# An adaLN block with linear attention and a mixture of experts: the opening reordered, and the output product in plain f32

## The reference

```
mod = silu(c) @ wmod                         # c: [4, 256], wmod: [256, 6*256]
sa, ca, ga, sb, cb, gb = six slices of mod   # one row of 256 per batch entry
ga, gb = sign * max(|.|, 0.25)
h = layernorm(x) * (1 + ca) + sa             # x: [4, 2048, 256]
q, k, v = h @ w_qkv.T, in 16 heads of 16;  q, k = elu(q)+1, elu(k)+1
S_t = S_{t-1} + k_t v_t^T;  z_t = z_{t-1} + k_t          # causal linear attention
o_t = (S_t q_t) / max(z_t q_t, 1e-6);  x = x + ga * (o @ w_out.T)
h = layernorm(x) * (1 + cb) + sb
top-2 of 8 experts (w_router), capacity 1280 rows each, gates renormalised
x = x + gb * sum_e combine_e * (silu(h @ w_gate.T) @ w_down[e].T)
```

## Time and profile before

| | |
|---|---|
| median of 3 runs | 967.09 us (965.5 to 968.11) |
| profiled execution | 968.82 us, span 967.1 us |
| mean granted TensorE clock | 0.962 of 2.4 GHz |
| PE, PEld busy | 880.2 us, 738.5 us |
| DVE, ACT, POOL busy | 644.7, 496.4, 515.3 us |

### The profile page before, as it was taken

The page is one execution under the profiler, slowest core; times in us unless marked ns, Lnnn a source line. Parts: engine busy times, 40 slices in busy tenths (PEclk is TensorE's granted clock), DMA queues, the critical chain, the costliest instruction groups (busy, mean ns, idle before and its releaser), DMA issues.

```text
span 967.1 us, 23422 instructions
## 1 busy us (share of the span) xinstructions
PE 880.2 (91%) x8232; PEld 738.5 (76%) x8232; DVE 644.7 (67%) x1869; ACT 496.4 (51%) x1002; POOL 515.3 (53%) x641
## 2 busy tenths in 40 slices
PE   4899999999999999999999999981099999999994
PEld 2677877777777777777787777751099999999994
DVE  4466587777867867778768677765056755677752
ACT  3645656655556555555565565332065555455541
POOL 3212435656556656565556564545535765566564
PEclk9899999999999999999999999995599999999998
DMA  9984012223222322222123211212156766676663
GB/s 320 338 268 106 2 45 89 67 90 95 59 87 65 103 93 65 87 75 58 64 50 76 56 36 44 52 29 72 53 144 148 153 128 138 142 140 142 135 110 43
DMA packets 70981, 98.36 MB, mean 102 GB/s; under 512 B 7794, under 2 KB 52850, under 8 KB 70792
## 3 DMA queue, kind: packets, MB, share of 16 engines
q1 hardware_dynamic: 37912, 52.09, 19.5%
q0 software_dynamic: 21760, 31.66, 14.9%
q10 hardware_dynamic: 11248, 13.81, 4.4%
HBM read 46.84 MB, written 63.36 MB: 114 GB/s over the span
## 4 chain that ended last, share of the span: by engine, by line
PE 80%; issue 5%; DVE 5%; POOL 4%; DMA 4%; ACT 1%; DVEq 0%; POOLq 0%; ACTq 0%; SPq 0%
PE SCW L1163 13%; PE SCW L1394 9%; PE PJ L1255 9%; PE OB L1196 7%; PE MD L1229 5%; PE OB L1187 5%; PE MA L1409 5%; PE MD L1409 4%; PE PJ L1265 4%; PE SB L1209 4%; PE MD L1173 3%; PE MA L1222 2%; DMA out<-EX,desti 2%; PE PJ L1280 2%; POOL slot_rows L480 2%
## 5 line engine op out<-in xcount | busy, mean ns | idle before, releaser
L825 DVE TENSOR_TENSOR Sm<-SCW,tri 128x1024 f32<-128x1024 f32 x128 | 156.1, 1220 | 75.5 <-PE SCW L1163 75.5
L480 POOL DMA_INDIRECT slot_rows<-Hrow,sloti x128 | 126.8, 991 | 43.2 <-issue 43.1
L1163 PE MATMUL SCW<-QM,KT 32*128 32x256 f32 x1024 | 144.9, 400 | 0.8 <-DVE Sm L825 0.3
L538 POOL DMA_INDIRECT out<-EX,desti x80 | 127.2, 1590 | 32.6 <-issue 32.2
L496 POOL TENSOR_TENSOR X<-X,og 128x256 f32 (+1 forms) x64 | 46.8, 731 | 174.8 <-DVE og L1024 174.2
L1163 PEld LDWEIGHTS SCW<-QM,KT 32*128 32x128 f32 x1024 | 87.7, 184 | 35.6 <-issue 19.6
L1255 PE MATMUL PJ<-hT,w_qkv 128*128 128x512 f32 x384 | 107.2, 417 | 6.1 <-POOL hT L490 6.1
L608 ACT ACTIVATE EX<-PJ 128x512 f32<-128x512 f32 x64 | 38.2, 597 | 103.3 <-PE PJ L1255 103.3
L1255 PEld LDWEIGHTS PJ<-hT,w_qkv 128*128 128x128 f32 x384 | 70.0, 195 | 18.4 <-issue 6.3
L490 POOL TENSOR_TENSOR hT<-N,hT 128x512 fp32r<-128x512 f32 x32 | 41.6, 1321 | 75.1 <-ACT hT L595 75.1
L1196 PE MATMUL OB<-Sm,VA 128*17 128x128 f32 x2048 | 81.1, 276 | 0.0
(11 more groups left out here) (191 smaller groups left out, 1986.7 us busy)
## 6 DMA issues: line engine op xcount, KB each, us to landing
Hrow<-slot_rows SPq DMA_DIRECT2D x32, 516.0 KB, 4.1
slot_rows<-erow ACTq DMA_DIRECT2D x1, 10400.0 KB, 52.4
X<-x SPq DMA_DIRECT2D x16, 512.0 KB, 4.9
out<-X SPq DMA_DIRECT2D x16, 512.0 KB
Hrow<-mod_rows SPq DMA_DIRECT2D x16, 512.0 KB, 8.0
QT<-slot_rows SPq DMA_DIRECT2D x8, 516.0 KB, 3.7
slot_rows<-Hrow,sloti POOLq DMA_INDIRECT x128, 2.8
N<-wd SPq DMA_DIRECT2D x4, 512.0 KB, 5.5
```

What stands on the lines that cost most here:

```text
L480: pool.indirect_dma_start(xe, bass.IndirectOffsetOnAxis(sloti[:, k, t:t + 1], 0), Hrow[:, 1 - gp, t, :], None, bounds_check=SLOTS - 1, oob ...
L538: pool.indirect_dma_start(out, bass.IndirectOffsetOnAxis(desti[s % 2][:, a:a + 1], 0), Ys[s % 2][:, a, :], None, bounds_check=TOK - 1, oob ...
L825: dve.tensor_tensor(o.rearrange("p c (k w) -> p c k w", k=2), SCW[:].rearrange("p k (c w) -> p c k w", c=DC), tri[:].rearrange("p k i -> p ...
L1163: last[k] = mm(SC[k][:, cc * 2 * P:(cc + 1) * 2 * P], KT[rows, gp, cc, q * P:(q + 1) * P], QM[rows, tp, :, cc, :], start=True, stop=True)
```

## The change

Seven things change.

1. Loads. `wmod` is loaded in two pieces: the columns of sa and ca on ScalarE's queue, the other two thirds on SP's queue between the two `X` loads. `wqkv` has a semaphore of its own, and is no longer behind the wait for `w_r`'s zeroing.
2. The slot fill is issued by ScalarE in its slot j = 4 instead of before Silu. Silu waits for `c` alone.
3. TensorE enters the slots after the columns of sa and ca; the modulation's four rows are made after the first group's transposes (j = 4), into PSUM banks `OB` and `SB` instead of the score banks, and VectorE copies them out after the low parts of `hT`.
4. The first group's low parts (`hT[:, 1]`) are made by VectorE instead of GpSimd.
5. ScalarE copies `saca` out after the first four norms (j = 3) instead of before `w_qkv`'s high part.
6. The output product uses plain f32: `ATs` and `w_o` have one part each, two matmuls instead of six; `attention_lo` is gone, as are `w_o`'s high and low part in the opening.
7. `mod12`, `tmp`, `sgn` and the experts' second block buffer lie elsewhere (`VS` is new); two waits for them fall away.

```diff
@@ buffers
-        ATs = sb("ATs", [P, 2, DC, P], F32R)
+        ATs = sb("ATs", [P, DC, P])
-        w_o = sb("w_o", [P, 2, DC, D], F32R)
+        w_o = sb("w_o", [P, DC, D])
+        VS = sb("VS", [P, 2, DC, BW], F32R)
-        mod12 = Smf[0:BATCH, DC * 6 * D:(DC * 6 + 4) * D].rearrange("p (k d) -> p k d", k=4)
-        tmp, sgn = (EX[0:BATCH, i, :].rearrange("p (k d) -> p k d", k=2) for i in range(2))
+        tmp, sgn = (KT[0:BATCH, 1, i, :].rearrange("p (k d) -> p k d", k=2) for i in range(2))
+        mod12 = Hf[0:BATCH, 2048:2048 + 4 * D].rearrange("p (k d) -> p k d", k=4)
@@ run_slots
-                    if early and it == -1 and j == early_at:
-                        early()
+                    if early and it == -1:
+                        early(j)
@@ SP
             sp.dma_start(X[:, 0:GT, :], xg[0]).then_inc(x_in[0], 16)
+            sp.dma_start(wmod_sb[:, :, 2 * D:6 * D], wmod[:, :, 2 * D:6 * D]).then_inc(wm_in[1], 16)
             sp.dma_start(X[:, GT:2 * GT, :], xg[1]).then_inc(x_in[1], 16)
...
-            sp.wait_ge(w_lo, 2)
+            sp.wait_ge(w_lo, 1)
@@ GpSimd
-                if q == 0 and group_ok(gn + 1):
+                if q == 0 and group_ok(gn + 1) and gn >= 0:
@@ ScalarE
             act.dma_start(cT[:], c).then_inc(c_in, 16)
-            act.dma_start(wmod_sb, wmod).then_inc(c_in, 16)
+            act.dma_start(wmod_sb[:, :, 0:2 * D], wmod[:, :, 0:2 * D]).then_inc(wm_in[0], 16)
+            act.dma_start(w_qkv_raw, wqkv).then_inc(wq_in, 16)
             act.wait_ge(wr_zero, 1)
-            for dst, src in ((w_qkv_raw, wqkv), (w_o_raw, wo), (w_r[:, :, 0:E], wr), (w_g_raw, wg)):
+            for dst, src in ((w_o[:], wo), (w_r[:, :, 0:E], wr), (w_g_raw, wg)):
                 act.dma_start(dst, src).then_inc(w_in, 16)
-            act.wait_ge(consts, N_CONST)
-            act.dma_start(xe[:, 0:D + 4]..., erow[:].to_broadcast(...)).then_inc(init_out, 16)
-            act.wait_ge(c_in, 32)
+            act.wait_ge(c_in, 16)
             act.activation(cS[:], cT[:], ACT.Silu).then_inc(c_silu, 1)
...
+            act.wait_ge(wq_in, 16)
+            act.activation(w_qkv[:, 0], w_qkv_raw, ACT.Copy).then_inc(w_hi, 1)
+            def early(j):
+                if j == 3:
+                    act.wait_ge(mod_mm, 1)
+                    (the two saca copies)
+                    act.wait_ge(mod_ev, 2)
+                if j == 4:
+                    act.wait_ge(w_in, 48)
+                    act.activation(w_g[:, 0], w_g_raw, ACT.Copy).then_inc(w_hi, 1)
+                    act.wait_ge(consts, N_CONST)
+                    act.dma_start(xe[:, 0:D + 4]..., erow[:].to_broadcast(...)).then_inc(init_out, 16)
...
-                if n_next == 0 and m == 0:
-                    act.wait_ge(gate_fix, 5)
@@ VectorE
+            def early(j):
+                if j == 0:
+                    (the parity column)
+                if j == 1:
+                    dve.wait_ge(w_hi, 1)
+                    (the low part of w_qkv)
+                if j == 4:
+                    for cidx in range(DC):
+                        dve.wait_ge(h_hi, cidx + 1)
+                        dve.tensor_tensor(hT[:, 1, cidx, :], hT_raw[:, cidx, :], hT[:, 0, cidx, :].bitcast(F32),
+                                          ALU.subtract).then_inc(h_lo, 1)
+                    dve.wait_ge(mod_mm, 3)
+                    (mod12 from OB and SB, then the clamping of the gates, as before)
+                if j == 7:
+                    dve.wait_ge(gate_fix, 5)
+                    dve.wait_ge(w_hi, 2)
+                    (the low part of w_g)
-                if tile_ok(n - 1):
-                    attention_lo(T)
@@ TensorE
             pe.wait_ge(c_silu, 1)
+            pe.wait_ge(wm_in[0], 16)
...
+            def early(j):
+                if j == 4:
+                    modulation(0)
+                    modulation(1)
+                if j == 7:
+                    pe.wait_ge(w_in, 48)
...
             def out_product(T):
-                pe.wait_ge(at_lo, T)
+                pe.wait_ge(at_done, T)
                 for cc in range(DC):
-                    for i, (ap, wp) in enumerate(SPLIT):
-                        last = mm(MD[:, 0:D], ATs[:, ap, cc, :], w_o[:, wp, cc, :], start=(cc + i == 0),
-                                  stop=(cc == DC - 1 and i == len(SPLIT) - 1))
+                    last = mm(MD[:, 0:D], ATs[:, cc, :], w_o[:, cc, :], start=(cc == 0), stop=(cc == DC - 1))
                 last.then_inc(op_full, 1)
```

More of the change, by code:

```diff
@@ L174, in adaln_block @@
         XT = [a.rearrange("p (k c n) -> p k c n", k=2, c=DC)
-              for a in (KS[:].rearrange("p k c n -> p (k c n)"), w_o[:].rearrange("p k c n -> p (k c n)"))]
+              for a in (KS[:].rearrange("p k c n -> p (k c n)"), VS[:].rearrange("p k c n -> p (k c n)"))]
         Ys = [EXf[:, i * 512:(i + 1) * 512].rearrange("p (a n) -> p a n", a=2) for i in range(2)]
@@ L790, in _ @@
             dve.memset(VA[:], 1.0).then_inc(dve_setup, 1)
[L791 to L816, removed]
@@ L818, in _ @@
-            SC0m, SC1m = (SC[k][0:BATCH, :].rearrange("p (k d) -> p k d", k=2) for k in range(2))
+            def early(j):
+                if j == 0:
+                    dve.wait_ge(consts, N_CONST)
+                    dve.tensor_reduce(parity[:, 0:1], pairmask[:], AX_X, ALU.add).then_inc(gate_fix, 1)
+                    dve.wait_ge(gate_fix, 1)
+                    dve.tensor_scalar(parity[:, 1:2], parity[:, 0:1], -1.0, 1.0, ALU.mult, ALU.add).then_inc(dve_setup, 1)
+                if j == 1:
+                    dve.wait_ge(w_hi, 1)
+                    dve.tensor_tensor(w_qkv[:, 1], w_qkv_raw, w_qkv[:, 0].bitcast(F32), ALU.subtract).then_inc(w_lo, 1)
+                if j == 4:
[4 more added lines that the diff above has]
+                    dve.wait_ge(mod_mm, 3)
+                    dve.tensor_copy(mod12[:, 0:2, :], OBm).then_inc(gate_fix, 1)
+                    dve.tensor_scalar(mod12[:, 2, :], SBm[:, 0, :], 1.0, None, ALU.add)
+                    dve.tensor_copy(mod12[:, 3, :], SBm[:, 1, :]).then_inc(gate_fix, 1)
+                    dve.wait_ge(gate_fix, 3)
+                    gate = mod12[:, 0:4:3, :]
+                    dve.scalar_tensor_tensor(tmp, gate, -1.0, gate, ALU.mult, ALU.max)
+                    dve.tensor_scalar(sgn, gate, 0.0, 2.0, ALU.is_ge, ALU.mult).then_inc(gate_fix, 1)
+                    dve.wait_ge(gate_fix, 4)
+                    dve.tensor_scalar(tmp, tmp, 0.25, None, ALU.max).then_inc(mb_ev, 1)
+                    dve.wait_ge(mb_ev, 1)
+                    dve.scalar_tensor_tensor(gate, sgn, -1.0, tmp, ALU.add, ALU.mult).then_inc(gate_fix, 1)
+                if j == 7:
+                    dve.wait_ge(gate_fix, 5)
+                    dve.wait_ge(w_hi, 2)
+                    dve.tensor_tensor(w_g[:, 1], w_g_raw, w_g[:, 0].bitcast(F32), ALU.subtract).then_inc(w_lo, 1)
@@ L820, in masked_scores @@
+            OBm, SBm = (a[0:BATCH, :].rearrange("p (k d) -> p k d", k=2) for a in (OB, SB))
             def masked_scores(T, pair, tp, n):
@@ L1141, in _, with modulation @@
             last.then_inc(mod_mm, 1)
-            for hh in range(2):
+            pe.wait_ge(dve_setup, 2)
+            pe.wait_ge(consts, N_CONST)
+            def modulation(hh):
+                if hh == 0:
+                    pe.wait_ge(wm_in[1], 16)
                 for k in range(DC):
-                    last = mm(SC[hh][0:BATCH, :], cS[:, k, :], wmod_sb[:, k, (2 + 2 * hh) * D:(4 + 2 * hh) * D],
+                    last = mm((OB, SB)[hh][0:BATCH, :], cS[:, k, :], wmod_sb[:, k, (2 + 2 * hh) * D:(4 + 2 * hh) * D],
                               start=(k == 0), stop=(k == DC - 1))
                 last.then_inc(mod_mm, 1)
-            pe.wait_ge(w_in, 64)
-            pe.wait_ge(dve_setup, 2)
-            pe.wait_ge(consts, N_CONST)
+            def early(j):
[4 more added lines that the diff above has]
+                    pe.wait_ge(w_in, 48)
             def scores(T, q, gp, tp, pair):
-                if isinstance(T, int) and T == 0 and pair == 0:
-                    pe.wait_ge(gate_fix, 3)
                 if pair == 0:
@@ L1246, in stage1_qk @@
                 if isinstance(G, int) and N == 0 and m == 0:
-                    pe.wait_ge(w_lo, 2)
+                    pe.wait_ge(w_lo, 1)
                 if m == 0:
```

38 lines of the change are left out of this document (17 added, 21 removed).

## The result

| | before | after |
|---|---|---|
| median (runs) | 967.66 us (6, 965.5 to 968.87) | 979.13 us (6, 974.78 to 984.58) |
| ratio, 95% interval | | 1.0128 (1.0092 to 1.0164) |
| profiled execution, its span | 968.82, 967.1 us | 983.63, 981.8 us |
| granted clock, mean | 0.962 | 0.958 |
| QK of group 0 starts | 27.02 | 21.03 |

The changed kernel is slower by 12.4 us by the ratio (8.9 to 15.9); the forecast was +9.0. In the two profiled executions the span grew by 14.7 us: 3.1 up to tile 2, 7.8 from tile 2 to tile 63, -0.5 from there to the experts, and 4.2 in the expert stage, which the diff does not touch except for one buffer's place. Without it the stages give 10.4 us, inside the interval of the ratio.

What follows compares the result with a forecast made beforehand. TensorE's instruction stream was taken to bound the attention stage, with waits only at its opening and end. +9.9 (tile loop) - 0.7 (end of attention) - 0.2 (opening) = +9.0 us on 967.09, so 976.1 us; range 968.5 to 982.

Steps and rivals of the forecast that it cites:

- TensorE's stream sets the loop: Attention tile loop: the stage is as long as TensorE's instruction stream, so freeing VectorE there buys nothing.
- The product, +9.9 a kernel: Output product in the tile loop: plain f32 costs +0.155 us in each of 64 tiles, +9.9 us (8.3 to 11.5).
- The -0.7 for the end of attention: End of attention: TensorE's two waits for `ATs` fall away, -0.7 us, bounds 0 and -1.5.
- The estimate after the Trainium skill: Output product: true FP32 as four passes, eight 256-column passes against six, 0.21 us more a tile, 13.6 us in all.
- The opening up to tile 0: Opening: QK starts at 22.1, 4.9 us earlier, and first scores come at 30.8, 7.7 us ahead.
- Rival 3: Opening: first piece of `wmod` lands with the whole, modulation at low clock, full 2.8 us paid; 981.9 us, chance 0.14.
- What is late next: Opening after tile 0: gate rows leave later, group 2 lands at 45.4, VectorE waits; 1.6 of 7.7 us are left.
- I keep 19.8: SP's queue in the opening: group 2 lands 19.8 us after the gate rows' store, as before.
- The clock: Opening, after TensorE's wait from about 42: the low clock costs 1.4 us, half of 2.8.
- The opening as a whole: Whole opening: -1.6 + 1.4 = -0.2 us (from -5 to +3).
- Rival 1: Opening: group 2 lands before 38 us, VectorE never waits, low clock not met again; 967.1 us, chance 0.12.
- Rival 4: Opening: it keeps 4.5 us, with gate rows at 23; 971.8 us, chance 0.20.

Runs made afterwards that it cites:

- pad: The changed kernel with VectorE again making one subtraction of 128x256 per tile, into a buffer nobody reads; 980.33 us, ratio 1.014.
- after_again: The changed kernel unchanged, run again beside other kernels on one chip; 981.24 us, ratio 1.0134.
- late_fill: The changed kernel with the slot fill issued after ScalarE's slot n = 2 instead of in j = 4; 968.63 us, ratio 0.9996.
- keep_busy: The changed kernel with 28 extra fp32r matmuls, result never read, on TensorE right before tile 1's second scores; 978.96 us, ratio 1.0126.

## Why the prediction was right, and which of its terms were off

It said 976.1, range 968.5 to 982, slower with 0.81; 979.13 came, 3.0 us more. The mechanism was the one forecast; two terms were off, in opposite directions.

- **TensorE's stream sets the loop: right.** 58 of 61 slots grew, in every quarter, and pad shows that VectorE's time was worth nothing.
- **The product, +9.9 a kernel: a slot is right, the sum too large.** The plain pass was put at 0.217 us; the successive starts give 0.215, and a slot grows by 0.15, as forecast. The step that was off is "Every one of the 64 tiles pays, as TensorE waits for nothing there". Three slots did not pay: the last two had waited for the low part, and the one from tile 23 to 24 for `An` (0.61 us). Together they give back 1.0 us inside the loop, where they would have paid 0.5. The list of waits behind the earlier trace rows has the wait for `An` (0.6 us, once), in a line that was not used; the second of the last two slots, where the product came 0.26 us late, is not in it at all. The -0.7 for the end of attention came as -0.4. Net the product is 7.7 us by the traces (7.9 in the loop, 0.2 ahead of it, -0.4 behind), against 9.2. The 4.0 us wait for `pos` in the earlier trace rows is the quarter-slot's own and did not change. The estimate after the Trainium skill, "FP8 and Floating Point Precision", TensorE Precision Notes, put the term at 13.6. Its four passes are borne out in their cost (two instructions of 0.215 us for 256 columns); it came out high since it took the fp32r passes at a bare 0.107 us where the rows have 0.118.
- **The opening up to tile 0: right.** QK at 21.03 (22.1), first scores at 29.86 (30.8). `wqkv` had landed at 10.1, 1.4 us sooner than assumed; the modulation's rows took 5.46 us (5.6). Rival 3's first condition, that the first piece of `wmod` lands with the whole, did not come: its product starts at 6.59, where before it started at 9.97.
- **What is late next: right in mechanism, and the terms off in one direction.** Store of the gate rows 24.73 (25.6), second scores of tile 1 49.28 (48.2), wait at group 2 as named. The term "I keep 19.8" from store to landing was 21.9: the store took 6.65 us to come through beside the fill, where it had been 5.1. It varies by execution, too: SP issued the broadcast between 31.4 and 33.9 in the five executions, of four kernels, that kept this order of queues and ran the fill from j = 4.
- **The clock: the term that was mis-sized.** "I take half, 1.4": it cost 3.55 us in this execution (9.02 - 5.31 - 0.155) and 2.8 in after_again, where the full price was put at 2.8. The opening as a whole was put at -0.2 and is +3.1 with the product's share. The lesson is in the choice, not the reading: the wait forecast here, 6 us, was as long as the one before that had been followed by the full price, and no row spoke for half of it.
- Product 1.5 too high and opening 3 too low: that the sum of the terms, 9.0, came nearer to the traces' 10.4 than the opening did to its own measure is luck. The other 1.6 us up to 979.13 belong to no term; the interval of the ratio is wider than that.
- Rival 1 (group 2 not late) describes what a later fill gives: in late_fill group 2 is there in time, and 968.6 came against the 967.1 worked out. Rival 4 names gate rows at 23 and a gain of 4.5; its own terms, with nothing paid for the clock, give 1.6 + 2.6 = 4.2.

## What to carry to other kernels

A reordering that makes compute ready sooner is worth what the next load allows: ask for each engine which data it will stand before at the new time, and which queue they come through. A bulk transfer with a late deadline is best issued after the urgent ones have passed: here it delayed a small store by 3 to 7 us and doubled the time of the loads behind it. And two changes in one diff should be timed apart: here the plain product cost 7 to 8 us and hid that the new opening, with the fill's issue moved, gains 7.

## What the runs showed that was not expected

- A store of 16 KB, until SP could go on, took 1.76 to 1.77 us in the four kernels that issue the fill later, and 5.1 (before) to 8.6 us (pad) in the nine executions that ran the fill beside it. Which part of its way is slow beside the fill is not shown.
- After the wait of 7.95 us, TensorE stayed at a granted 0.5 until 57.1, 7.8 us after it had resumed; before, the low stretch ended at 32.9, 5.9 us after QK had started. The price follows that time: 3.55 us for 7.8, 2.8 for 6.1 (after_again), 1.6 for the 3.4 of keep_busy.
- A plain f32 matmul of 256 columns is two instructions 0.215 us apart, an fp32r one of 256 columns one of 0.118: three fp32r products cost less (0.71) than the one plain product they stand for (0.86).
